# Bringing the split expert weights back from HBM in six transfers of 1 MB instead of three of 2 MB

## What is computed

```
x = x + tanh(g_xattn) * (attention(layernorm(x) Wq, ctx Wk, ctx Wv; 8 heads of 64) Wo + bo)
h = layernorm(x)
logits = h gate_w                     # 8 experts, the best 2 of each token, softmax of the two
y_e = (silu(h Wu[e]) * (h Wv[e])) Wo[e]     # Wu, Wv: 8 x 512 x 128; Wo: 8 x 128 x 512
x = x + tanh(g_ffn) * sum over the chosen 2 of w_k * y_e
```

## Time and profile before

| | us |
|---|---|
| median of 3 runs | 1108.74 |
| lowest and highest of the 3 | 1103.36, 1109.86 |
| the profiled execution, its own time | 1095.86 |
| its span in the profile | 1094.1 |

### The profile page before, as it was taken

How to read it: one execution, slowest core, us unless ns; L and a number is a source line. 1 busy time by engine, 2 the same in 40 slices (tenths; PEclk the granted TensorE clock), 3 DMA queues, 4 the chain that set the end, 5 groups by cost and what they waited for, 6 DMA issues and landing times.

```text
span 1094.1 us, 22759 instructions
## 1 busy us (share of the span) xinstructions
PE 902.0 (82%) x8210; PEld 546.8 (50%) x8210; DVE 677.7 (62%) x1595; ACT 570.5 (52%) x1022; POOL 536.3 (49%) x645
## 2 busy tenths in 40 slices
PE   4888878998899899899899989886650899799890
PEld 2344435555455455455555545443320777677660
DVE  5687757777777767767777776586234454344440
ACT  4366646566556656556655656456210465555450
POOL 6122324253465366447546543645563146666564
PEclk9999989999999999999999999998665899999995
DMA  8555773422362264254336228334343588999996
GB/s 274 154 161 158 236 244 78 141 73 74 97 199 71 65 199 112 60 177 112 76 88 208 67 63 266 95 93 146 97 142 105 151 195 170 181 195 194 185 159 81
DMA packets 125325, 154.26 MB, mean 141 GB/s; under 512 B 48288, under 2 KB 81056, under 8 KB 124832
## 3 DMA queue, kind: packets, MB, share of 16 engines
q1 hardware_dynamic: 108352, 115.40, 36.0%
q0 software_dynamic: 16864, 37.40, 17.8%
HBM read 62.83 MB, written 56.30 MB: 109 GB/s over the span
## 4 chain that ended last, share of the span: by engine, by line
PE 51%; DVE 12%; DMA 11%; issue 9%; ACT 7%; POOL 6%; SPq 2%; POOLq 1%; ACTq 0%; DVEq 0%
PE G L1233 26%; DMA out_dram<-V,Ph 7%; PE MX L1275 4%; PE ST L1290 3%; PE ST L1289 3%; PE MX L1457 3%; PE G L1242 3%; POOL out_dram L662 2%; PE PV L1302 2%; PE PV L1304 2%; PE PV L1306 2%; DVE tiles L863 2%; DVE mx L873 2%; POOL expert_rows L576 2%; PE G L1449 1%
## 5 line engine op out<-in xcount | busy, mean ns | idle before, releaser
L619 POOL TENSOR_TENSOR Pl<-P,Ph 128x512 f16<-128x512 f32 x128 | 150.6, 1184 | 223.5 <-ACT Ph L697 223.0
L694 ACT ACTIVATE P<-ST 128x512 f32<-128x512 f32 x256 | 153.3, 599 | 203.3 <-PE ST L1290 194.4
L873 DVE TENSOR_REDUCE mx<-MX 128x1 f32<-128x512 f32 x256 | 168.1, 684 | 26.4 <-PE MX L1275 26.4
L697 ACT ACTIVATE Ph<-ST 128x512 f16<-128x512 f32 x256 | 154.6, 604 | 0.4
L662 POOL DMA_INDIRECT out_dram<-V,Ph x78 | 122.5, 1571 | 48.1 <-ACT V L830 28.4
L1457 PE MATMUL MX<-heads,tiles 128*128 128x256 f16 x936 | 119.8, 280 | 16.5 <-DVE heads L1187 16.3
L1302 PE MATMUL PV<-V,Ph 128*128 128x65 f16 x1024 | 114.2, 196 | 23.0 <-issue 23.0
L1302 PEld LDWEIGHTS PV<-V,Ph 128*128 128x128 f16 x1024 | 97.9, 98 | 43.8 <-issue 26.2
L1304 PE MATMUL PV<-V,Ph 128*128 128x64 f16 x1024 | 114.5, 197 | 0.0
L1306 PE MATMUL PV<-V,Pl 128*128 128x65 f16 x1024 | 114.1, 195 | 0.0
L1457 PEld LDWEIGHTS MX<-heads,tiles 128*128 x936 | 91.5, 100 | 38.6 <-issue 21.3
(11 more groups left out here) (206 smaller groups left out, 1917.6 us busy)
## 6 DMA issues: line engine op xcount, KB each, us to landing
heads<-expert_rows SPq DMA_DIRECT2D x39, 516.0 KB, 5.5
tiles<-in_x_dram SPq DMA_DIRECT2D x32, 256.0 KB, 4.8
tiles<-in_ctx_dram SPq DMA_DIRECT2D x32, 256.0 KB, 5.2
second_norm<-in_x_dram SPq DMA_DIRECT2D x32, 256.0 KB, 3.2
out_dram<-second_norm SPq DMA_DIRECT2D x32, 256.0 KB, 2.4
heads<-q_hi SPq DMA_DIRECT2D x124, 64.0 KB, 2.0
heads<-k_hi SPq DMA_DIRECT2D x124, 64.0 KB, 2.0
expert_rows<-second_norm SPq DMA_DIRECT2D x2, 2064.0 KB, 11.0
```

The lines of the kernel that those rows point to most:

```text
L619: nc.gpsimd.tensor_tensor(Pl[:, hh, c, :], P32[:, c, :], Ph[:, hh, c, :], ALU.subtract).then_inc(pl_pool, 1)
L694: nc.scalar.activation(P32[:, c, :], ST[:, c % 2, :], ACT.Exp, scale=0.125 / SC2).then_inc(p_ready, 1)
L697: nc.scalar.activation(Ph[:, hh, c, :], ST[:, c % 2, :], ACT.Exp, scale=0.125 / SC2).then_inc(ph_ready, 1)
L873: nc.vector.tensor_reduce(out=mx[:, k // TT, k % TT:k % TT + 1], in_=MX[:, (k + odd) % 2, :], axis=AXX, op=ALU.max).then_inc(mx_taken, 1)
```

## The change

`load_split` takes a part (0 or 1) and moves that half of the tensor, 1 MB. The six halves are issued at these places: u hi at the end of step 26 and u lo at the start of step 27; v hi at the end of step 27 and v lo at the start of step 28; o hi at the start of step 30 and o lo at the end of step 30. A half at the start of a step is issued ahead of that step's `load_residual`. The waits on `filled` and on the stores of the pieces stay with the first of each. Each tensor's semaphore now counts two transfers, so PE waits for 32 in place of 16. The view of four slabs at once (`fw_slab`) is gone.

```diff
-        fw_slab = {n: slab(4 * i, 4) for i, n in enumerate("uvo")}
...
-            def load_split(n):
-                sp.dma_start(fw_slab[n], fw_dram[n].rearrange("p a e d -> p (a e d)")).then_inc(fw_back[n], 16)
+            def load_split(n, a):
+                sp.dma_start(FW[n][a].rearrange("p e d -> p (e d)"),
+                             fw_dram[n][:, a].rearrange("p e d -> p (e d)")).then_inc(fw_back[n], 16)
...
                 if b == 0:
                     for i in range(3 * j, 3 * j + 3):
                         load_piece(i)
+                if g == STEPS - 5:
+                    load_split("u", 1)
+                if g == STEPS - 4:
+                    load_split("v", 1)
+                if g == STEPS - 2:
+                    sp.wait_ge(filled, use["k", STEPS - 3] + 1)
+                    load_split("o", 0)
...
                 if g == STEPS - 6:
                     sp.wait_ge(filled, use["k", g - 1] + 1)
                     sp.wait_ge(filled, use["c", TILES - 1] + 1)
-                    for n in "uv":
-                        sp.wait_ge(fw_st[0], len(PIECES) // 3 * 16)
-                        sp.wait_ge(fw_st[1], len(PIECES) // 3 * 16)
-                        sp.wait_ge(fw_st[2], len(PIECES) // 3 * 16)
-                        load_split(n)
+                    for k in range(3):
+                        sp.wait_ge(fw_st[k], len(PIECES) // 3 * 16)
+                    load_split("u", 0)
+                if g == STEPS - 5:
+                    load_split("v", 0)
                 if g == STEPS - 2:
-                    sp.wait_ge(filled, use["k", STEPS - 3] + 1)
-                    load_split("o")
+                    load_split("o", 1)
...
             for n in "uvo":
-                pe.wait_ge(fw_back[n], 16)
+                pe.wait_ge(fw_back[n], 32)
```

## The result

| | before | after |
|---|---|---|
| median, us (20 runs each) | 1103.23 | 1099.13 |
| lowest and highest, us | 1095.86, 1109.86 | 1088.86, 1105.71 |
| span of the profiled execution, us | 1094.1 | 1092.3 |

The ratio of after to before is 0.9947 [0.9924, 0.997] at 95%. Two later repetitions, on other chips, gave 0.9937 [0.9912, 0.9962] and 0.9939 [0.9915, 0.9963]. The mean of the three is 0.9941, some 6.5 us of 1100: a gain of 0.6%, real but under 1%. The forecast was 9.9 us, and 1098.8 us for the time.

A forecast was written before the change was run, and what follows sets the result against it. The prediction took PE to be stalled by POOL's waits for residual tiles queued behind bulk loads of u, v and o. Terms 6.5 - 0 - 0.2 + 3.6 = 9.9 us, off 1108.74, gave 1098.8 us, range 1091 to 1105.

The forecast's parts named there:

- Step 27: With only u's halves ahead of the residual, PE's stall before its weighted head and the clock fall go: 6.5 us won.
- Step 28: v's halves newly stand ahead of this step's residual; POOL still finishes 0.7 us before PE needs it: cost 0.
- Step 30: o hi goes out ahead of the residual, making POOL's remainders 0.2 us late for PE; the row stores don't move.
- Step 31: Only o lo, 1 MB and not 2, stands ahead of the residual: 3.6 us won, bounds 2 and 4.2.
- 1 MB less is 3.8: In step 31, the residual lands 3.8 us earlier, from the second 2 MB of u and v taking 7.6 us.
- everything behind it shifts with it: After `row_lo` in step 31, row stores, second head's remainders, last weighted head and tail all come 3.6 to 3.9 us earlier.
- The last attention step ends less than 8 us earlier: Sign in the trace after that the prediction is wrong: the end of attention gains under 8 us.
- The rule weighed: A skill's transfer cost, 2.0 us fixed plus bytes at 436 GB/s, applied to each half: step 28 2 us later, sum about 7.
- (a): Rival: each half pays a fixed part, 2.8 us more per pair in steps 27 and 28; 3.8 us back, 1102.6; chance 0.15.
- (b): Rival: transfer time goes by the number of queued transfers, not bytes; 12.1 us slower, 1120.8; chance 0.04.
- (c): Rival: only step 27's stall is real, a later wait absorbs step 31's 3.6; gain 6.3, 1102.4; chance 0.13.
- (d): Rival: unprofiled runs have slower transfers, so the stalls removed are longer; 3 us more gain, 1095.6; chance 0.17.

The follow-up runs named there:

- The third megabyte: The changed kernel with u lo loaded once more behind the pair of v, ahead of step 28's residual; one execution, 1087.32 us.
- four halves: The changed kernel with u and v in halves, all issued at the end of step 26 ahead of step 27's residual; ratio to before 0.9993.

## Why the prediction was right, and where it was not

The forecast was a gain under 1% and 1098.8 us, and the result is 1099.13. But the two times agree better than the sum did: it had 9.9 us, the ratios give 6.5 and the stage 7.5.

- **Step 27, +6.5: right.** Measured 6.3. The pair of halves behaves as a whole u did. In the third profile of the kernel after the residual was there for `add_bias` at 676.05 (forecast 677.4), POOL was through at 679.6 and PE came at 683.28 (forecast 683.4). The pause and the fall of the clock after it both went. The pause alone had been 5.2, 5.0 and 4.2 us in the three profiles before, 4.8 on average, so the 1.3 us for the clock was rightly counted.
- **Step 28, 0 with a margin of 0.7: right, and as narrow as told.** The rows of that profile, first POOL's, then PE's:

```profile
699.37 1.27 POOL L569 TENSOR_TENSOR second_norm<-second_norm,tgbo 128x512 f32<-128x512 f32 x1 [7.83 <-DMA second_norm<-in_x_dram]
700.59 2.28 POOL L625 TENSOR_TENSOR Pl<-P,Ph 128x512 f16<-128x512 f32 x2
```

```profile
703.38 0.19 PE L1308 MATMUL PV<-V,Ph 128*128 128x65 f16 x1
```

  The forecast had 699.3, 702.8 and 703.5; these are 699.4, 702.9 and 703.4, a margin of 0.5. The third megabyte showed what is on the other side of it.
- **Step 30, -0.2: right in effect, for a reason half told.** The residual landed 6.2 to 6.3 us after o hi's issue in each profile (742.93 less 736.63 in the first), a little earlier than the forecast's 6.9. The stretch to mark 30 lost 0.8 all the same. The term left out that the remainders, once late, run at the same time as DVE's small operations ahead of the maxima; see the last section. But PE's second head of step 30 waits for POOL, whose row stores "don't move", as the prediction said: by that head the kernel after is 0.1 us behind.
- **Step 31, +3.6: the step that failed.** Measured from the second head of step 30 it brought 1.7 us. Two parts of the step were wrong.

  The first is "1 MB less is 3.8", taken from u and v. From o's issue to `add_bias` it took 11.5, 11.8 and 11.7 us in the three profiles before, 9.5, 9.7 and 9.1 after, so 1 MB less saved 2.2. o lo landed 7.5, 8.2 and 6.4 us after its issue, where o whole had taken 10.3, 10.6 and 10.6; that is 3.1 less, the figure that the prediction had from 336 GB/s. Of that 0.9 was lost behind it: the residual was there 1.5 to 2.7 us after o lo, where it had been there 1.1 to 1.2 after o. In the first profile of the kernel after, from its DMA issues around 753 us:

```profile
tiles<-fo_split SPq DMA_DIRECT2D x1, 1024.0 KB, 7.5
```

  PE's pause went from 4.5, 3.7 and 4.1 to 1.9, 2.3 and 1.7, not under 1. The 3.8 came from v, the second 2 MB, which ran when the row stores of its step had been issued over 11 us before (and v took 6.9 and 6.7 us in the repeats, not 7.6). Around o lo, issued at 752.96, POOL issues the four row stores of step 30, some 258 KB each (749.7 to 754.8 us). Place matters: in these three profiles o hi, at the start of the step, landed in 5.4 to 5.6 us and o lo, at its end, in 6.4 to 8.2. That the row stores are the reason is argued, not shown: no run had o lo ahead of step 31's residual and the stores moved.

  The second is "everything behind it shifts with it". PE came to its first head of step 31 2.6 us earlier (8.8 us after the second head of step 30 and not 11.5), and about 1 us of that was gone by the end of the last head. From the first to the last head, with POOL's row stores and remainders between, it took 9.1 us in each profile before and 9.5 in each after. And in both later profiles of the kernel after the pause ahead of the last head was 4.87 us, and the head ran at a granted clock of 0.50. PE's row and the window of the last head (columns as in the earlier trace rows), first of the kernel before, second profile, then of the kernel after, third profile:

```profile
777.39 0.19 PE L1302 MATMUL PV<-V,Ph 128*128 128x65 f16 x1 [2.73 <-issue]
777.39:779.10 1.71, 1.62 (x48) 1.50 (x48) 0.05 (x1) 0.00 (x0) 1.44 (x5) 1.00 0.32 118
```

```profile
766.35 0.22 PE L1308 MATMUL PV<-V,Ph 128*128 128x65 f16 x1 [4.87 <-issue]
766.35:769.20 2.85, 2.77 (x48) 2.61 (x48) 0.04 (x1) 0.00 (x0) 2.52 (x5) 0.50 0.03 6
```

  So part of what PE won it waited out again before the last head, and in these two the last head took 1.1 us longer. In the two first profiles the pause was 3.1 us and the head's clock 0.62 before, 3.2 us and 1.00 after; on average the pause grew from 2.9 to 4.3 us and head and result took 0.5 us longer. The 1.7 us is under the lower bound given (2, "the row stores take bandwidth"); the table's 2.4 is within it only because it takes in what mark 30 had lost.
- **The sum.** "The last attention step ends less than 8 us earlier" was named as a sign of error. It came 7.5 earlier on average, 9.1 in the pair of profiles laid side by side above. By that line the sum was off by a quarter: 1.8 of the missing 2.4 us for the two terms of o, the other 0.6 for the stretch 26 to 27, which is the pauses of one profile.
- **The rule weighed.** The prediction sets a sum of about 7 us beside its own. The Trainium skill, "DMA: Bandwidth & Descriptors", section "Anatomy of one DMA", gives that fit of 2.0 us and 436 GB/s for transfers issued from GpSimd, and the halves are issued from SP. The 7 is nearer to the measured 6.5 and 7.5 than 9.9 is, but by luck: it had step 28 late, and step 28 lost nothing; what fell short was step 31.
- **The rivals.** (a), a fixed part for each half, needed over 11.9 us between issue and landing; the pairs took 9.1 to 12.1 (688.55 less 676.49 in the second profile, the longest and just over it), no pause came, and four halves landed no later than two wholes. (b), slower, fell in the same way. (c), only the first stall real, is not what happened: step 31 gave 1.7 of its 3.6, 1.6 with step 30's loss. (d), more than summed, fell. The total, some 6 to 7 us, is close to (c)'s 6.3 by number, and that shows how little a total says of a mechanism.
- **The level.** The forecast took 9.9 from 1108.74, the median of three runs. With 20 runs the kernel before was at 1103.23. The time came out right because two errors met: a start 5.5 us too high and a gain 5.8 too large by the two medians (3.4 by the ratios).

## What to carry to other kernels

When a bulk load shares a queue with a small load that a compute chain waits for, look at what stands ahead of the small one: issue the small one first, and only then ask whether the bulk needs cutting. Don't add up waits. Compare the longest with the slack of the engine that is fed; a change that leaves the sum alone can be worth 6 us, and one that removes two thirds of it nothing. Take a price per megabyte from the stretch in which it is to be used: the 3.8 us of one stretch were 2.2 in another. And ask of every pause that goes whether the next one grows: here one did.

## What the runs showed of the hardware that was not expected

**Order in the queue.** A 256 KB tile landed 17.5 us after its own issue behind 4 MB (16.7 and 15.9 in the repeats), 14.8 behind four halves (its issue is later there; from the first half it is 18.3), 12.8 behind 3 MB, 8.0 to 11.2 behind 2 MB, 5.6 to 5.7 behind 1 MB in step 30 and 7.1 to 8.8 in step 31. With both halves of o right behind it and none ahead it was 2.5 us, in step 27 with u behind it 3.6 to 4.4. The Trainium skill, "DMA: Bandwidth & Descriptors", section "Queues, rings and completion order", says that each DMA engine takes the descriptors of a ring in the order in which they were queued; the trace agrees.

**A DVE operation held by POOL.** With o hi ahead of the residual, POOL's remainders fall on the moment at which DVE negates the maxima, before the transposed maxima that PE waits for. The operation (`mneg`, 128 x 8), in the third profile of the kernel before and then of the kernel after, followed by PE's row behind it:

```profile
750.08 0.17 DVE L878 TENSOR_SCALAR mneg<-mx 128x8 f32<-128x8 f32 x1
```

```profile
737.43 0.93 DVE L884 TENSOR_SCALAR mneg<-mx 128x8 f32<-128x8 f32 x1
```

```profile
738.41 0.27 PE L1286 MATMUL MX<-identity,mneg 128*8 128x128 f32 x1 [0.91 <-DVE mneg L884]
```

0.17 us became 0.93, and PE stood 0.91 us for it. The two remainders, from 735.61, took 2.72 us, where a pair takes 2.27 in step 31, and end at 738.33, DVE's operation at 738.36. It was 0.93 in all five profiles with o hi ahead of the residual (the kernel after, the third megabyte, the four halves at once); in the three before it was 0.61, 0.17 and 0.17, and 0.17 to 0.50 in the six other kernels. That is 0.6 of the 0.8 us that the stretch to mark 30 lost, on average; the rest is DVE's own remainder and maxima ahead of it, and differs from profile to profile. The Trainium skill, "SBUF — State Buffer", section "SBUF: two separate sides", describes a pair of ports that VectorE and GpSimd can only hold in turn, each for a whole instruction; the trace agrees in so far as the one waited out the other. The section says it of VectorE operations in a 2-port mode or with two SBUF inputs; in which mode this one ran, no trace here shows.

**The same step at another clock.** In the first steps, which no kernel here changes, one and the same piece of work took 17.7 us at a granted clock of 1.00 in nine profiles and 19.4 to 21.0 us at 0.91 to 0.84 in the other five, among them one of the kernel before and one of the kernel after. The window from 46 to 68 us of the kernel after, second profile and then third:

```profile
46.00:68.00 22.00, 17.50 (x66) 6.84 (x64) 13.16 (x25) 8.97 (x17) 2.31 (x2) 0.84 0.35 96
```

```profile
46.00:68.00 22.00, 16.33 (x98) 7.46 (x97) 16.56 (x30) 12.36 (x23) 2.31 (x2) 1.00 0.37 103
```

That is the execution's doing and not the program's, and its 3.3 us are half of what the change is worth. It is why a term of 2 us was read from three profiles of each kernel and not from one.
